# Stage of pairs: rows of X scaled on ScalarE during the search, and the layer's offset added to X in the second edge sum

## What is computed

```python
x = x + gnn0(LN(x))      # edge sum of x@W, batch normalisation, relu
x = x + ffn0(LN(x)[None])[0]
x = x + gnn1(LN(x))      # edge sum, two products, normalisation * scale + offset
x = x + moe(LN(x)[None])[0]   # top 2 of 8 experts

# ffn0 on h = LN(x): it returns processed + h
weights = h @ wr + br
_, idx = top_k(weights, k);  sel_idx = idx[:, :k - 1]       # about half of the rows
y = gelu(sel @ w1 + b1) @ w2 + b2
processed = zeros.at[sel_idx].set(y * w_sel)

# gnn1 on feat = LN(x)
aggr = segment_sum(edge_val[:, None] * feat[edge_col], edge_row) + (1 + eps) * feat
h = relu(relu(aggr @ W1 + b1) @ W2 + b2)
return (h - mean) * scale * rsqrt(var + 1e-10) + offset
```

## Time and profile before

| | |
|---|---|
| median of 3 runs | 3527.38 us (3525.95 to 3528.80) |
| profiled execution: span from first to last instruction | 3521.7 us |
| busy, share of the span: TensorE | 2647.4 us, 75% |
| VectorE | 2613.3 us, 74% |
| ScalarE | 1008.4 us, 29% |
| GpSimd | 2208.3 us, 63% |
| stage of pairs (start to barrier) | about 1387 to 1785 us |
| second edge sum | about 1785 to 2798 us |
| mean granted TensorE clock | 0.868 |

### The profile page before, as it was taken

One profiled execution on the slowest core, in us unless ns is written; L12 is line 12 of the kernel. 1 busy time (PEld: TensorE's weight loads), 2 busy tenths in 40 slices (PEclk: granted clock), 3 DMA queues, 4 the chain that ended last, 5 costly groups with the idle time before them and its releaser, 6 DMA issues. The chain is left out here.

```text
span 3521.7 us, 55765 instructions
## 1 busy us (share of the span) xinstructions
PE 2647.4 (75%) x15311; PEld 2239.6 (64%) x15311; DVE 2613.3 (74%) x6603; ACT 1008.4 (29%) x2073; POOL 2208.3 (63%) x2147
## 2 busy tenths in 40 slices
PE   6888466666666665899967677777776569999998
PEld 4777344454444444789945555555555459999997
DVE  6999566666666666969967777777777778888886
ACT  0011000000000002545511111111111168888886
POOL 0455577777777774345557777777777326666664
PEclk9999687878878787899978888888788779999999
DMA  3011433333333332000133333333333447776775
GB/s 98 10 44 33 120 105 105 105 105 105 105 105 105 105 105 73 1 2 31 37 103 111 113 112 111 113 113 111 113 111 113 133 134 216 213 218 211 219 211 140
DMA packets 164679, 389.01 MB, mean 110 GB/s; under 512 B 46378, under 2 KB 95602, under 8 KB 151019
## 3 DMA queue, kind: packets, MB, share of 16 engines
q0 software_dynamic: 99072, 233.49, 24.4%
q1 hardware_dynamic: 65387, 152.94, 12.8%
HBM read 343.97 MB, written 42.98 MB: 110 GB/s over the span
## 5 line engine op out<-in xcount | busy, mean ns | idle before, releaser
L1081 POOL DMA_INDIRECT g_got<-table,e_source x1568 | 1492.1, 952 | 506.5 <-issue 458.9
L1174 PE MATMUL psum<-g_got,g_route 128*128 x3328 | 1087.2, 485 | 642.0 <-DMA g_got<-table,e_source 253.6
L1174 PEld LDWEIGHTS psum<-g_got,g_route 128*128 128x128 f32 x3328 | 760.9, 239 | 888.4 <-issue 763.5
L1107 DVE TENSOR_TENSOR A<-A,psum 128x256 f32 x1664 | 698.5, 420 | 523.6 <-PE psum L1174 345.1
L1090 DVE TENSOR_SCALAR g_route<-columns,e_local,e_weight 128x128 f32<-128x128 f32 x1664 | 472.5, 363 | 17.7 <-issue 12.9
L368 POOL DMA_INDIRECT records<-rec,place x120 | 148.7, 1239 | 220.6 <-ACT rec L580 122.0
L1582 POOL TENSOR_TENSOR f_ht_lo<-f_ht,f_ht_hi 128x512 fp32r<-128x512 f32 x100 | 133.7, 1341 | 187.8 <-ACT f_ht_hi L1531 182.1
L142 PE MATMUL psum<-e_xt_hi,e_w_hi 128*128 128x256 f32 x832 | 238.0, 286 | 5.5 <-issue 5.3
L142 PE MATMUL psum<-e_w_hi,e_ht_hi 128*128 128x256 f32 x832 | 233.1, 280 | 3.1 <-DVE e_w_lo L1981 3.1
L144 PE MATMUL psum<-e_xt_hi,e_w_lo 128*128 128x256 f32 x832 | 233.8, 281 | 0.0
L143 PE MATMUL psum<-e_xt_lo,e_w_hi 128*128 128x256 f32 x832 | 233.7, 281 | 0.0
(11 more groups left out here) (420 smaller groups left out, 5198.5 us busy)
## 6 DMA issues: line engine op xcount, KB each, us to landing
e_w<-in_m_w SPq DMA_DIRECT2D x104, 1024.0 KB, 5.0
g_got<-table,e_source POOLq DMA_INDIRECT x1568, 2.8
expert_table<-g_normal SPq DMA_DIRECT2D x52, 128.0 KB
table<-xn SPq DMA_DIRECT2D x49, 128.0 KB, 1.7
X<-in_x SPq DMA_DIRECT2D x1, 6144.0 KB
table<-f_ring SPq DMA_DIRECT2D x24, 256.0 KB, 2.1
out<-X SPq DMA_DIRECT2D x1, 6144.0 KB
f_w<-in_f_w SPq DMA_DIRECT2D x2, 1024.0 KB, 7.3
```

The source lines that it names most:

```text
L1081: pool.indirect_dma_start(got[:, c % RING, :], None, rows, bass.IndirectOffsetOnAxis(ap=source[:, c:c + 1].bitcast(U32), axis=0)).then_inc ...
L1107: dve.tensor_tensor(to, to, sums_of(c), ALU.add).then_inc(added, 1)
L1174: ins = pe.matmul(sums_of(c), route[:, c % (GB + GSEM), :], row(got, at[j % GSEM]), start=True, stop=True)
```

## The change

It does four things.

1. The two operations that make -mean*rstd and rstd+1 (L1667, L1668 before) stand ahead of the search instead of behind it, and signal `scales_known`.
2. The 49 operations X*(rstd+1) - mean*rstd leave VectorE (L1673 before) and are done by ScalarE as ACTIVATE Identity with a scale and a bias per row (L1548 after), 8 tiles per unit in the units 6 to 12: 3 ahead of the wait for the tile j = 0 and 5 ahead of that for j = 1. VectorE waits for their count (`x_scaled`).
3. X + offset leaves `normalise_made` (L1693 before, 25 operations), and the load of `offset` leaves the stage of pairs.
4. In the second edge sum `offset` is an eighth parameter array, and `add` begins with X + offset for the tile that the step finishes (L930 after, 52 operations of 128x256), with a `done`, ahead of its wait for the root.

```diff
@@ -830,8 +830,8 @@
         class GraphTiles:
-            LOADS = 7
-            PER_TILE = 5
+            LOADS = 8
+            PER_TILE = 6
             PER_LN = 3
@@ -848,7 +848,7 @@
                 self.b1, self.b2 = here("b1", [P, KD]), here("b2", [1, D])
-                self.scale = here("scale", [P, D])
+                self.scale, self.offset = here("scale", [P, D]), here("offset", [P, D])
                 self.xt, self.hidden = here("xt", [P, KD, P]), here("hidden", [P, KD, P])
@@ -864,6 +864,7 @@
                 sp.dma_start(self.scale[:], g1_scale.partition_broadcast(P)).then_inc(self.loaded, 16)
+                sp.dma_start(self.offset[:], g1_offset.partition_broadcast(P)).then_inc(self.loaded, 16)
                 sp.dma_start(self.wr[:], m_wr.rearrange("(k p) n -> p k n", p=P)).then_inc(self.loaded, 16)
@@ -924,6 +925,9 @@
                 done = self.steps_of(dve, k, 3)
+                if k == 0:
+                    dve.wait_ge(self.loaded, self.LOADS * 16)
+                done(dve.tensor_tensor(row(X, t), row(X, t), self.offset[:], ALU.add))
                 dve.wait_ge(self.root_ready, k + 1)
@@ -1272,7 +1276,7 @@
             gain, shift, root = here("gain", [P, KD]), here("shift", [P, KD]), here("root", [P, KD])
-            wr, eps1, offset = f0_wr, f0_eps, f0_wr
+            wr, eps1 = f0_wr, f0_eps
             ring = here("ring", [P, 4, D])
@@ -1283,11 +1287,12 @@
             DIGITS = 15
+            SCALED, SCALED_FIRST = 8, 3
             MAGIC = 0x5F3759DF
...
             loaded = sem("f0_loaded")
-            SECOND_WEIGHTS, OFFSET, LATER_FIELDS = 16, 32, 80
+            SECOND_WEIGHTS, LATER_FIELDS = 16, 64
             high, low = sem("f0_weights_hi"), sem("f0_weights_lo")
@@ -1295,6 +1300,7 @@
             counted, counted_all = sem("topk_counted"), sem("topk_all")
+            scales_known, x_scaled = sem("f0_scales_known"), sem("f0_x_scaled")
             row_ready, landed, stored = sem("t1_row_ready"), sem("t1_landed"), sem("t1_stored")
@@ -1400,8 +1406,6 @@
                 sp.dma_start(w2[:].rearrange("p (k n) -> p k n", k=HB), f0_w2.rearrange("(k p) n -> p k n", p=P)).then_inc(loaded, 16)
-                sp.wait_ge(counted, 1)
-                sp.dma_start(offset[:], g1_offset.partition_broadcast(P)).then_inc(loaded, 16)
                 table_rows = table[1].rearrange("(t p) d -> p t d", p=P)
@@ -1535,9 +1539,18 @@
 
+                def scale_rows(m, j):
+
+                    first = SCALED * (m - NORM_STEPS) + j * SCALED_FIRST
+                    if 0 <= first < NT:
+                        act.wait_ge(scales_known, 1)
+                        for t in range(first, min(NT, first + (SCALED_FIRST, SCALED - SCALED_FIRST)[j])):
+                            act.activation(X[:, t, :], X[:, t, :], ACT.Identity, bias=moments[:, t, 0:1], scale=rstd[:, t:t + 1]).then_inc(x_scaled, 1)
+
                 def keep_made(m):
...
                     for j in range(2):
+                        scale_rows(m, j)
                         act.wait_ge(made, 2 * m + (j + 1))
@@ -1662,16 +1675,13 @@
                 s(dve.tensor_scalar(wgt[:], wgt[:], f0_br_row[:, 0:1], None, ALU.add))
+                s(dve.scalar_tensor_tensor(moments[:, :, 0], moments[:, :, 0], -1.0, rstd[:], ALU.mult, ALU.mult))
+                dve.tensor_scalar(rstd[:], rstd[:], 1.0, None, ALU.add).then_inc(scales_known, 1)
                 topk.search(dve, s)
-
-                s(dve.scalar_tensor_tensor(moments[:, :, 0], moments[:, :, 0], -1.0, rstd[:], ALU.mult, ALU.mult))
-                s(dve.tensor_scalar(rstd[:], rstd[:], 1.0, None, ALU.add))
 
...
                     tiles = tiles_in(m)
-                    for t in tiles:
-                        ins = dve.tensor_scalar(X[:, t, :], X[:, t, :], rstd[:, t:t + 1], moments[:, t, 0:1], ALU.mult, ALU.add)
-                    s(ins)
+                    dve.wait_ge(x_scaled, tiles.stop)
                     for t in tiles:
@@ -1690,9 +1700,7 @@
                     s(dve.tensor_scalar(pair_of(A, m), normal_of(m), eps1[:, 0:1], None, ALU.mult))
-                    s(dve.tensor_tensor(pair_of(X, m), pair_of(X, m), offset[:].unsqueeze(1).to_broadcast([P, len(tiles), D]), ALU.add))
-
-                dve.wait_ge(loaded, OFFSET)
+
                 ends = [*range(PER_STEP, UNITS - PER_STEP, PER_STEP), UNITS - 3, UNITS - 1, UNITS]
```

## The result

The changed kernel takes **3532.54 us** in the median (3528.11 to 3539.52, 18 runs), the kernel before beside it 3525.86 us. The ratio is **1.0019, 95% interval 1.0013 to 1.0026**: some 7 us more where the prediction had 1.9 us less, and outside its range. The profiled execution has a span of 3531.0 us against 3521.7, so 9.3 us more; the medians differ by 6.7.

What follows compares the result with a forecast made beforehand. TensorE bounds the stage of pairs until VectorE's tail, GpSimd's gathers the second edge sum. Terms of -0.45 and -1.44 us, the rest 0, give -1.9 us: 3527.4 to 3525.5 us, range 3521 to 3530.5 us for 8 in 10.

Steps and rivals of the forecast that it cites:

- the offset in the second edge sum: 0 for 52 steps: Second edge sum: 52 VectorE additions, 0.57 us a step, make 18.29 us, below GpSimd's 18.95, so they cost 0.
- the sign that the prediction named: Second edge sum: the forecast is wrong if GpSimd's period between gathers rises from 1.257 us.
- Rival 1: Second edge sum: the addition holds up GpSimd's gathers, +19.9 us or a smaller cost; chance 0.04 and 0.06.
- small price: Second edge sum: gathers held 0.075 us per addition, 3.9 us in all, total 3529.4 us; chance 0.06.
- slower from 0.17 us an operation: Second edge sum: the hold per added addition from which the kernel would count as slower.
- The full price: Second edge sum: each addition holds gathers for its whole 0.42 us, 21.8 us in all, total 3547.3 us; chance 0.04.
- The term of 0: Search: two small operations push the first count by 0.4 us, covered by VectorE's 2.93 us wait for its answer.
- The tail: End of the stage of pairs, VectorE alone: -0.45 us from scaling and -1.44 us from the offset, -1.9 us together.
- rival 4: Stage of pairs: ScalarE's rows at 0.8 us delay TensorE, up to +5 - 1.9, 3530.5 us; chance 0.04.
- rival 3: Second edge sum: VectorE becomes the bound, 31 us less 1.9, total 3556 us; chance 0.03.
- rival 5: Stage of pairs: VectorE's backlog ends late in most runs, so unloading it gains some 8 us, 3519 us; chance 0.05.
- Rival 2: Search: TensorE's clock stays up (total change -5.5 us) or drops further (+1.7 us); chance 0.07 each.

Runs made afterwards that it cites:

- statistics instead: Kernel before with X scaled on ScalarE, plus an unused one-SBUF-operand bn_stats where the change puts its addition; ratio 1.0006, on a slower chip 1.0010.
- offset alone: Kernel before with only the offset's load and addition moved to the second edge sum, X still scaled on VectorE; ratio 1.0009, on a slower chip 0.9990.
- scaling alone: Changed kernel with the offset's load and addition back in the stage of pairs; ratio 0.9997, on a chip where every kernel was some 12% slower.

## Why the prediction was wrong

**The step that failed** is the last but one of the sum, "the offset in the second edge sum: 0 for 52 steps". It asked whether VectorE still keeps up with GpSimd. It does: its waits for TensorE from 1910 to 2745 us fell from 69.8 to 53.4 us (1.2 us a step, forecast 1.0). But the addition costs GpSimd's own time, and the sign that the prediction named, a longer period of the gathers, is there: 992.8 / 783 = 1.268 us instead of 1.257. Measured: 9.3 us of held gathers more, 0.18 us for each of the 52 additions. Of this 0.08 lies under the addition and 0.10 under other operations; part of that follows from the addition's holds, and how large a part isn't shown.

**How the bound went wrong.** Rival 1 named the mechanism and gave it 0.10 in all. It judged against it by "neither seems to hold up the other", from a median of 947 ns, and bounded its small price at 0.075 us an operation by spreading the excess of all gathers over all 104 operations with two SBUF operands. The excess isn't spread. It was 46 gathers of 784 even then, and 15 of these lay under the two operations with two SBUF operands, 0.12 us each (10 of 140 and 5 of 89 ns in the mean). That only 16 gathers started under the centring's 52 holds for that kernel alone; the changed one has 29. An estimate from these rows, with every addition hit, would have been 52 x 0.12 = 6 us for the addition, and as much again for each neighbour that it moves. By the traces the point named as decisive, "slower from 0.17 us an operation", was just reached; the medians' 6.7 us lie just below the 7 us that stand behind it. The full price, 0.42 us an operation, didn't occur: the most that a gather lost under an addition of the changed kernel was 0.22 us (1.164 instead of 0.945).

**A row read past.** The earlier trace rows give L1693 a median of 693 and a maximum of 1672 ns: one addition of two SBUF operands, 24 times of the same size. Five of them took 1.67 us, and each of these began inside a subtraction on GpSimd, which has two SBUF operands too; no other did. Two from the kernel before, VectorE and GpSimd:

```profile
1610.87 1.67 DVE L1693 TENSOR_TENSOR X<-X,f_wr 128x512 f32<-128x512 f32 x1
...
1633.01 0.69 DVE L1693 TENSOR_TENSOR X<-X,f_wr 128x512 f32<-128x512 f32 x1
```

```profile
1610.69 1.30 POOL L1582 TENSOR_TENSOR f_ht_lo<-f_ht,f_ht_hi 128x512 fp32r<-128x512 f32 x1
...
1633.28 1.58 POOL L1582 TENSOR_TENSOR f_ht_lo<-f_ht,f_ht_hi 128x512 fp32r<-128x512 f32 x1 [5.76 <-ACT f_ht_hi L1531]
```

The addition of 1610.87 begins within the subtraction and ends 0.55 us after it. That of 1633.01 began first and keeps its 0.69 us, and the subtraction takes 1.58 us instead of 1.30. So the trace of before did show that the two engines hold each other up, in another stage. It showed it in the second edge sum too. The prediction looked at L929, which never passed 505 ns; the other operation with two SBUF operands, the centring, did:

```profile
L921 DVE SCALAR_TENSOR_TENSOR g_centred<-g_result,g_mean_var,g_scale x52: 483/485/546, 1842.9 to 2790.8; 128x256 f32<-128x256 f32 x52
```

Three of the 52 took 525 to 546 ns, each with a gather that started less than 0.1 us after it. In the changed kernel the same is plain in the two small operations moved ahead of the search:

```profile
1511.51 1.35 DVE L1678 SCALAR_TENSOR_TENSOR row_numbers<-row_numbers,rstd 128x49 f32<-128x49 f32 x1
1512.89 1.18 DVE L1679 TENSOR_SCALAR rstd<-rstd 128x49 f32<-128x49 f32 x1
...
1511.49 1.30 POOL L1595 TENSOR_TENSOR f_ht_lo<-f_ht,f_ht_hi 128x512 fp32r<-128x512 f32 x1 [0.59 <-ACT f_ht_hi L1535]
1512.74 1.28 POOL L1585 TENSOR_TENSOR f_xt_lo<-A,f_xt_hi 128x512 fp32r<-128x512 f32 x1
```

They took 1.35 and 1.18 us where the first took 0.213 behind the search. The forecast had 0.4 us for both; it was 2.5. The term of 0 held nevertheless: the answer to the first count came 131.55 us after the stage's first Relu, before 131.45.

**What was right.** The tail: 1.9 us. The parts also came out singly, measured from the same copy to the end of the last normalised row: about 0.5 us for the scaling (statistics instead, predicted 0.45) and 1.5 for the offset (offset alone, predicted 1.44). ScalarE's rows fitted by the margins named, so rival 4 didn't occur. VectorE never became the bound (rival 3), and no gain came beyond the tail from the 29 + 17 us that left VectorE (rival 5): TensorE waited for nothing from 1566 to 1785 us, as before.

**Rival 2** occurs in some executions. Three rows of the stretch 1515 to 1566 us (columns as in the earlier trace rows, the clock last but two): the changed kernel, the same again, the kernel before again.

```profile
1515.00:1566.00 51.00, 44.56 (x328) 42.25 (x327) 31.64 (x62) 29.23 (x61) 19.77 (x15) 0.93 0.00 1
```

```profile
1515.00:1566.00 51.00, 44.57 (x348) 42.08 (x347) 31.79 (x63) 29.77 (x63) 19.74 (x15) 1.00 0.00 1
```

```profile
1515.00:1566.00 51.00, 44.60 (x325) 42.02 (x324) 29.98 (x57) 21.43 (x46) 19.73 (x15) 0.93 0.02 3
```

With the granted clock at 1.00 of full speed throughout (2.4 GHz) TensorE's last count of the search began 3.0 us earlier, 178.3 us after the stage's first Relu instead of 181.3. The two traces of the kernel before have 0.93. One program gave both values, so whether the change makes the higher one more frequent is open. The scaled rows aren't needed for it: offset alone, without them, has 0.97 in the same 51 us of its search.

**What the skill says.** Against the rows here: the Trainium skill ("SBUF — State Buffer", section "SBUF: two separate sides") has a VectorE operation with two SBUF inputs and a GpSimd operation that reads SBUF lock each other out: whichever starts first keeps the ports for its whole length. The trace agrees that it is an exclusive hold in both directions (centrings of 526 to 548 ns where the gather was first) and that a PSUM operand avoids it. It differs in the extent: with a gather of 0.945 us on GpSimd only its first 0.12 us are exposed (a gather that the addition outlasted by 0.32 us took 1.142, and 0.32 - 0.197 = 0.12), and an operation with two SBUF operands that began later in the gather, L933 at 1973.45, took its usual 0.48 us.

## What to carry to other kernels

Where GpSimd's gathers set a stage, count VectorE's free time, but also count its operations with two SBUF operands: each can hold a gather that starts under it, and here a constant operand (a scale, an offset) held in PSUM removed that at no cost in the operation. Read the mean of a group of equal instructions beside its median: a mean above it, or a maximum like 1672 ns beside a median of 693, can be a few instructions that were held, and it doesn't say how many will be after a change. Compare starts: what runs at the moment when the long ones begin?

## What was unexpected of the hardware

- Only the start of a gather is sensitive. Under one-operand statistics or a sum of SBUF and PSUM (L1111, 241 gathers in the changed kernel, mean 945 ns) nothing is held; under the addition 29 of 32.
- A single-operand operation can hold as well: the route operations L1094 (128x128, SBUF to SBUF, no second tensor) held 30 of 183 gathers in the changed kernel by some 75 ns each, nearly always what was left of the operation's 0.34 us less 0.13 us.
- Holds can chain. One hold of 0.1 to 0.2 us often puts the fifth gather after it under the centring. With an addition of 0.425 us the held time grew by 0.18 us a step, not by the 0.08 that it holds itself, and with two additions it was less than with one (9.4 against 13.2 and 11.7 us).
- On the chip on which the kernels took some 3950 us, the edge sums and the work right behind them were longer; the stage of pairs was not (396.3 us, scaling alone).
